# Preparing expert weights in rank order inside the first expert stage of a macaron block (mixture of experts, state space scan, mixture of experts)

## The reference, cut to what matters

```
x: 4096 tokens x 256, float32
ffn(h):  router logits = h @ Wr (8 experts); expert = argmax; p = largest softmax value
         out = p * (gelu(h @ W1[expert] + b1[expert]) @ W2[expert] + b2[expert])
         W1: 8 x 256 x 1024, W2: 8 x 1024 x 256
ssm(h):  h_t = a*h_{t-1} + B u_t (complex, 128 states), y = Re(C h), over 4096 steps
x = x + 0.5*ffn(layernorm(x))
x = x + ssm(layernorm(x))
x = x + 0.5*ffn(layernorm(x))
```

## Time and profile before

| | |
|---|---|
| runs | 741.01 us median of 3 (734.8 to 749.26) |
| profiled execution, first to last instruction | 743.5 us (the profile gives no other time of its own) |
| PE busy | 589.5 us, 79% |
| DVE busy | 531.1 us, 71% |
| ACT busy | 396.8 us, 53% |
| POOL busy | 330.0 us, 44% |
| mean granted TensorE clock | 0.869 of full speed |

### The profile page before, as it was taken

How to read it: one execution, slowest core, us unless ns; L and a number is a source line. 1 busy time by engine, 2 the same in 40 slices (tenths; PEclk the granted TensorE clock), 3 DMA queues, 4 the chain that set the end, 5 groups by cost and what they waited for, 6 DMA issues and landing times.

```text
span 743.5 us, 18466 instructions
## 1 busy us (share of the span) xinstructions
PE 589.5 (79%) x6396; PEld 518.0 (70%) x6396; DVE 531.1 (71%) x1204; ACT 396.8 (53%) x879; POOL 330.0 (44%) x310
## 2 busy tenths in 40 slices
PE   5960149999999899994477878139999999999997
PEld 5950138998888787893245657129998778988886
DVE  5869967778886775784499993927776666766675
ACT  4877846565554555552336653107555546546463
POOL 0031183555545453531477881162555454554532
PEclk9555559999999999998658895558999999999999
DMA  8993031111111111113102211030111111111210
GB/s 276 374 375 122 5 99 31 40 45 43 49 45 38 35 51 37 38 30 99 51 29 90 80 57 57 1 103 19 44 51 44 36 50 36 45 41 36 50 36 2
DMA packets 34872, 51.86 MB, mean 70 GB/s; under 512 B 6747, under 2 KB 27933, under 8 KB 34528
## 3 DMA queue, kind: packets, MB, share of 16 engines
q1 hardware_dynamic: 24800, 31.90, 12.6%
q0 software_dynamic: 9984, 18.79, 9.0%
HBM read 37.95 MB, written 14.55 MB: 71 GB/s over the span
## 4 chain that ended last, share of the span: by engine, by line
PE 68%; DVE 18%; issue 7%; DMA 3%; ACT 2%; POOL 1%; SPq 1%; ACTq 0%; POOLq 0%; DVEq 0%
PE bank L1065 31%; PE bank L1082 9%; PE bank L1083 9%; PE bank L1084 9%; PE bank L982 4%; PE bank L1041 3%; DVE stats L580 3%; DVE weights_arena L613 2%; PE bank L976 2%; DMA weights_arena<-L_attn_u 2%; DVE weights_arena L920 1%; DVE weights_arena L757 1%; DVE weights_arena L917 1%; DVE weights_arena L942 1%; DVE ev L927 1%
## 5 line engine op out<-in xcount | busy, mean ns | idle before, releaser
L519 ACT ACTIVATE weights_arena<-bank,b1t,inv 128x128 f32<-128x128 f32 x624 | 228.4, 467 | 211.2 <-PE bank L1065 161.2
L1065 PE MATMUL bank<-weights_arena 128*128 128x128 f16 x3744 | 239.2, 222 | 23.5 <-issue 17.5
L1065 PEld LDWEIGHTS bank<-weights_arena 128*128 x3744 | 220.6, 99 | 39.8 <-issue 37.0
L1082 PE MATMUL bank<-weights_arena 128*128 x624 | 170.2, 273 | 1.2 <-issue 1.0
L1083 PE MATMUL bank<-weights_arena 128*128 x624 | 170.1, 273 | 1.3 <-issue 1.1
L1084 PE MATMUL bank<-weights_arena 128*128 x624 | 170.1, 273 | 0.9 <-issue 0.6
L816 DVE TENSOR_SCALAR weights_arena<-weights_arena,hscale 128x512 f16<-128x512 f32 x156 | 76.8, 492 | 83.6 <-ACT weights_arena L519 77.4
L819 DVE SCALAR_TENSOR_TENSOR weights_arena<-weights_arena,hscale 128x512 f16<-128x512 f32 x156 | 117.3, 752 | 5.6
L375 POOL DMA_INDIRECT recf<-records,sorti x78 | 81.4, 1043 | 23.8 <-issue 23.8
L381 POOL DMA_INDIRECT out<-weights_arena,sorti x39 | 39.5, 1013 | 112.7 <-DVE weights_arena L835 99.8
L381 POOL DMA_INDIRECT x_after_ffn<-weights_arena,sorti x39 | 40.6, 1040 | 105.3 <-DVE weights_arena L835 95.8
(11 more groups left out here) (181 smaller groups left out, 702.0 us busy)
## 6 DMA issues: line engine op xcount, KB each, us to landing
weights_arena<-L_ffn_W SPq DMA_DIRECT2D x16, 1024.0 KB, 12.6
...
recf<-records,sorti POOLq DMA_INDIRECT x78
weights_arena<-L_attn_u,sorti POOLq DMA_INDIRECT x39
x_after_ffn<-weights_arena,sorti POOLq DMA_INDIRECT x39
```

The lines of the kernel that those rows point to most:

```text
L519: last = act.activation(hb[q % 2][:, f, :], src, ACT.Gelu, bias=b1t[:, bass.ds(e * FC + f, 1)], scale=inv1[:, bass.ds(e, 1)])
L1065: last = pe.matmul(acc[:, f * P:(f + 1) * P], weights[wpart * DC + d], xts[q % 2][:, xpart, d, :], start=(n == 0), stop=(n == 5))
L1082: pe.matmul(acc, hs[q % 2][:, 0, f, :], high, start=(f == 0), stop=False)
```

## The change

The experts are ranked by their number of tiles, the largest first, in the first routing (`route_count(1)`), and everything about weights is then held by rank, not by expert. The tiles of `ffn(1)` lie in rank order; `ffn(2)` maps its experts to ranks in `route_owners(2)`. Weights are loaded by rank: SP reads the table `order` and issues the loads of ranks 0 and 1 when it is there, and those of rank r when the low parts of rank r-2 are done. b1 is loaded with each expert (element by element into its transposed place), b2 in eight pieces.

Only rank 0 is prepared ahead of `ffn(1)`. Rank r is prepared in tiles 4(r-1)-2 to 4r-2 of `ffn(1)`: ACT runs one of `row_sums` or `high_part` after the gelus of each tile (`prepare`), and DVE runs `weight_scales`, `low_part` of W1, `bounds_up` with `low_part` of W2, and `product_scales` in successive tiles. So 14 of the 16 low parts move into tiles of `ffn(1)`. The nine `double` and two `readout` calls move out of them to the entry. In both expert stages DVE's steps are interleaved in another way, and PE's `product2` waits for the first half of the result two tiles earlier rather than the second.

The core of the diff:

```diff
-LAG = 4
+LAG = 2
@@ sync engine
-            for c in (1, 2):
+            for c in range(1, NC):
                 load_x(c)
-            for e in range(E):
...
+            def load_expert(r):
+                e = sp.value_load(order[0:1, r:r + 1], min_val=0, max_val=E - 1)
+                sp.dma_start(raw(r, 0)..., W1[bass.ds(e, 1)]...).then_inc(wload[2 * r], 16)
+                sp.dma_start(raw(r, 1), W2[bass.ds(e, 1)]...).then_inc(wload[2 * r + 1], 16)
+                sp.dma_start(b1t[:, r * FC:(r + 1) * FC], B1[bass.ds(e, 1)]...,
+                             allow_slow_non_contiguous=True).then_inc(wload[2 * r + 1], 16)
...
+            sp.wait_ge(order_done, 1)
+            load_expert(0)
+            load_expert(1)
             store_records(1)
             load_b2(1)
+            for r in range(2, E):
+                sp.wait_ge(w_lo, 2 * r - 2)
+                load_expert(r)
@@ scalar engine
+            def prepare(k):
+                if 0 <= k < 4 * (E - 1):
+                    (row_sums if k % 4 < 2 else high_part)(1 + k // 4, k % 2)
...
+                if ph == 1:
+                    row_sums(0, 0)
+                    row_sums(0, 1)
+                    high_part(0, 0)
+                    high_part(0, 1)
...
                 norm(0)
                 norm(1)
+                if ph == 1:
+                    prepare(0)
+                    prepare(1)
                 for q in range(NT):
                     if q + 2 < NT:
                         norm(q + 2)
+                    if ph == 1 and q % 4 == 0 and q < 4 * E:
+                        act.wait_ge(inv_done, q // 4 + 1)
...
+                    if ph == 1:
+                        prepare(q + 2)
@@ vector engine, the tile loop
+                for q in range(-2, NT):
+                    r = (q + 4) // 4
+                    weighs = ph == 1 and 1 <= r < E
+                    if weighs and q % 4 == 1:
+                        bounds_up(r)
+                    if weighs and q % 4 == 2 and q > 0:
+                        product_scales(r)
                     if q + 2 < NT:
+                        split_x(q + 2, 0)
...
                     if q + 1 < NT:
+                        split_h(q + 1, 0, 0)
+                    if ph == 1 and q % 4 == 3 and 1 <= (q + 5) // 4 < E:
+                        weight_scales((q + 5) // 4)
+                    if q + 2 < NT:
+                        split_x(q + 2, 1)
+                    if q + 1 < NT:
+                        split_h(q + 1, 0, 1)
+                        split_h(q + 1, 1, 0)
+                        if weighs and q >= 0 and q % 4 < 2:
+                            low_part(r, q % 4)
+                        split_h(q + 1, 1, 1)
+                    if q >= 0:
+                        result(q)
+                        residual(q)
@@ tensor engine: ffn, product1, product2, the tile loop
-                if ph == 1:
-                    pe.wait_ge(w_lo, NW)
+                    if ph == 1 and q % 4 == 0 and q < 4 * E:
+                        pe.wait_ge(w_lo, q // 2 + 1)
-                        pe.wait_ge(s["o"], q - 1)
+                        pe.wait_ge(s["o_chain"], q - 1)
...
+                    if weighs and q % 4 == 0:
+                        pe.wait_ge(s["xt"], q + 3)
+                        bounds_turned(r)
+                    if weighs and q % 4 == 1:
+                        pe.wait_ge(s["xt"], q + 3)
+                        bounds_all(r)
```

338 lines of the change are left out of this document (163 added, 175 removed).

## The result

The changed kernel took 762.32 us (median of 6 runs, 752.59 to 773.44), the kernel before 738.62 us (6 runs, 732.59 to 749.26) beside it: 1.0252 of before, 95% interval 1.017 to 1.0333. The forecast was 729, with 746 as its upper end.

What follows compares the result with a forecast made beforehand. DVE was taken to bound the entry and PE the expert stages, passing to DVE in 28 tiles. Terms -22, +2.5 and +7 sum to -12.5 us: 728.5, say 729, against the 741.0 median; range 712 to 746.

Steps and rivals of the forecast that it cites:

- The sum: Whole kernel: -22 us at the start, +2.5 first tile, +7 in 28 tiles, together -12.5 us.
- 28 tiles: ffn(1) tiles with weight work: DVE needs 6.3 us a tile, taken as 6.4 against PE's 6.15: +7 us.
- Entry: Before ffn(1): logits to sorted tokens in 24.5 us, sorted at 70.9, 18.4 us earlier; doublings hidden in DVE's wait.
- the two prices: Load of b1 by element: 60 or 107 ns a packet, costing nothing at the first or 2.4 us at the second.
- Start to logits: Start of the kernel: PE's 1.38 us wait for x goes, so logits are complete at 46.4.
- First tile: Start of ffn(1): ACT's two sums of rank 1 ahead of the first gelu cost 0 to 4.2 us, taken as +2.5.
- can borrow from the light one: ffn(1): DVE's heavy tiles (7.0, 6.5, 6.5 us) borrow from the light one (5.1), within about 4 us.
- rival 2: ffn(1): no borrowing between tiles, 6.9 us a tile, +21 us, 742.5 us in total; chance 0.24.
- The rest: Waits for scales, later loads, second routing's extra step and PE's earlier release in ffn(2): nothing for all.
- its sign of being wrong: Second expert stage or scan changing by more than 3 us would show the prediction wrong where it left nothing.
- Rival 4: Entry: PE at twice its rate throughout, counted as faster than 726.2 us; chance 0.04.

Runs made afterwards that it cites:

- e14: Kernel before with only the change's order of DVE tile steps and PE's earlier release, in both expert stages: 0.998 of before.
- e3: Changed kernel with b2 stored once in rank order and loaded by one broadcast for ffn(2), not in eight loads: 1.023 of before.
- e18: Changed kernel with product scales on POOL ahead of scatter, low parts halved over all tiles, b2 in one load, first-tile sums and split x early: 0.993 of before.
- e8: Changed kernel with PE's small bounds products waiting for the previous tile's result instead of a later split x: 1.031 of before.
- e2: Changed kernel with ACT's two sums of rank 1 ahead of the norms of tiles 0 and 1: 1.021 of before.
- e10: Changed kernel with ACT's sums for ranks 1 to 7 over an eighth of each matrix: 1.032 of before.
- e6: Changed kernel run again without any edit: 1.026 of before.
- e1: Changed kernel with DVE's low step of split x right behind its high step, in both expert stages: 1.023 of before.
- e13: Changed kernel with the old order of DVE tile steps and PE's old wait for the whole result, in both stages: 1.026 of before.
- e7: Changed kernel with the 14 low parts cut into pieces and spread over all four tiles of a rank: 1.011 of before.
- e16: Changed kernel with the edits of e7 and e3 together: 1.012 of before.

## Why the prediction was wrong, by its steps

**The sum.** Forecast -12.5 us, measured +28.1 in the profiled pair. Of the 40.6 us between them 4.2 lie ahead of the first product, 4.0 in the first tile, 11.5 in the tiles up to result 27, and 21.0 behind it, where the sum had nothing. In the quiet pair (e14, e3: +12.7) 24.7 of 25.2 us lie in the tiles up to result 27. So the 28 tiles are the step that failed in each pair; in the first pair the second stage failed beside it.

**Entry: right.** Logits to sorted 24.0 us (forecast 24.5), to the first product 13.0 (11.1): 19 us gained in each of the three pairs, beside 20.6 forecast for this part. The doublings were hidden. b1 was there in time but for 1.62 us of ACT's wait, ahead of scales that the routing on DVE hid. It had landed 17.5 us after the logits (49.10 to 66.61), where the first of the two prices gave 20.1 and the second 23.1. In 57 to 72 us the queue moved 4746 packets in 92.1% of 16 engines' 15 us, 47 ns each; that is a mean over elements and the packets of the matrices, so the price of an element alone isn't shown. That the load goes by element shows in the packets: those under 512 bytes rise from 6747 in the trace of before to 15275 in the changed kernel's, by 8528, where b1 of eight ranks has 8192 elements; here they lay beside other work.

**Start to logits: luck.** The forecast was 46.4; with the changed kernel's entry it came between 42.7 (e18) and 49.5 (e8). What differs is PE's rate: in the trace of before the first two chunks' 16 matmuls took 1.96 and 2.59 us, in the changed kernel's each chunk's took 3.42 (in e3 1.92 and 1.85, then 2.77). So the wait of 1.38 us for x went, and the logits were later all the same.

**First tile: mis-sized and not a term of its own.** +2.5 forecast (0 to 4.2), +5.4 to +6.5 measured to the first result. The reason for the term, the sums of rank 1 ahead of gelu, isn't what costs: with the sums out of the way the first result came 17.6 us after the first product (e2; e3 17.3), with an eighth of them 19.9 (e10; e6 20.4). In e2 ACT waited for gathered records instead. And e1 and e13, where PE's second product is on time, and e2, where the sums are out of the way, reach result 27 no earlier. What a first tile saves is lost where DVE falls behind a few tiles later.

**28 tiles: the step that failed.** I put DVE's need at 6.3 us a tile, which the trace confirms, and took 6.4 since heavy tiles "can borrow from the light one". They borrow too little. I counted a tile from result to result, with the product scales in a tile of their own (7.05, 6.54, 6.45, 6.15). But PE is waiting for split x, and from split x to split x bounds and scales fall into the same stretches as the low parts: 8.2, 8.6, 4.5, 6.3. Two such in a row are more than PE's lead of one tile, and PE waits 2 us for split x. That is rival 2, at 6.9 us a tile: measured 6.75 to 6.9. Rival 2 had no term for the slower product that follows such a wait in four of e3's seven: 4.4 to 4.5 us instead of 2.85. e7 shows the size of both: with the heaviest tile at 7.0 us instead of 7.4, four take 25.9. Even rival 2's total, 742.5 us, is 20 under the measured median.

The other half of the error is the tile that I compared with. I took before's 6.15 us as PE's pace, with gaps that a slower DVE would partly fill. In the quiet group the pace without weights in the tiles is 5.56 (e14), 22.2 us for four. Against it DVE's own 25.2 (4 x 6.3) costs 3.0 us for each rank, and the measured 27.0 costs 4.8; e7's 25.9 costs 3.7. Seven ranks at 4.8 are 33 us, beside 31.7 in the third pair, while 19 / 7 = 2.7 us is what a rank's leaving the entry brought. By this estimate even perfect borrowing had nothing to win.

**The rest, at nothing.** Wrong in the first pair: +21.0 us behind result 27, of which `ffn(2)`'s 38 tiles are 13.0, and the forecast had named 3 us there as its sign of being wrong. True in the quiet pair: order, release, b2 and routing add up to 0.6 us. In the other two pairs `ffn(2)` got 4 to 13 us longer by pairs of 9 and 4.4 us. e14, e13 and e16 exclude the order and b2 only where such pairs don't occur. Whether the changed kernel has more of them than before, or the executions profiled happened to, is open.

**Rival 4.** Its 0.04 stands for a PE at twice its rate through the whole entry, and no run shows that. In the first pair nothing of it occurred: each chunk's 16 matmuls took 3.42 us in the changed kernel, logits at 49.1. In e3 and e13 a small part did: two chunks at nearly twice the rate (1.92 and 1.85 us in both), logits at 43.1 and 43.0 us.
